# Reordering the setup of a four-layer cross-attention kernel on one core

## What is computed

```python
x = L0(x, ctx)        # layernorm of x and ctx, 8 heads, residual
x = L1(x, ctx, mask)  # 16 heads, causal and key padding mask, residual
x = L2(x, ctx)        # 16 heads, output projection, MLP with tanh gelu
x = L3(x, ctx, pad)   # masked self attention, cross attention, MLP, layernorms
```

## Time and profile before

| | us |
|---|---|
| median of 3 runs | 562.75 |
| lowest and highest | 554.84, 569.61 |
| the profiled execution | 558.87 |
| its span, first to last instruction | 557.1 |
| PE, DVE, ACT, POOL busy | 486.3, 407.6, 329.0, 263.4 |
| mean granted PE clock | 0.932 |

### The profile page before, as it was taken

One profiled execution on the slowest core, in us unless ns is written; L12 is line 12 of the kernel. 1 busy time (PEld: TensorE's weight loads), 2 busy tenths in 40 slices (PEclk: granted clock), 3 DMA queues, 4 the chain that ended last, 5 costly groups with the idle time before them and its releaser, 6 DMA issues.

```text
span 557.1 us, 16733 instructions
## 1 busy us (share of the span) xinstructions
PE 486.3 (87%) x6464; PEld 299.2 (54%) x6464; DVE 407.6 (73%) x1093; ACT 329.0 (59%) x662; POOL 263.4 (47%) x334
## 2 busy tenths in 40 slices
PE   1548876799999878899999999999999999999973
PEld 1436554455555544455666666565555556666652
DVE  6267876645688886687888877778878897788452
ACT  1424655433556554467777766656666767888851
POOL 3585776824666774524344433334333533422243
PEclk9977889965799996799999999999999999999998
DMA  4593323332233332232223322232333332220000
GB/s 112 99 274 100 103 60 96 81 72 62 64 68 86 76 78 54 59 77 69 69 67 69 69 62 60 54 70 63 77 69 85 80 79 60 69 62 14 13 20 19
DMA packets 72021, 40.68 MB, mean 73 GB/s; under 512 B 7016, under 2 KB 71560, under 8 KB 71816
## 3 DMA queue, kind: packets, MB, share of 16 engines
q1 hardware_dynamic: 71944, 39.61, 30.1%
HBM read 5.00 MB, written 1.05 MB: 11 GB/s over the span
## 4 chain that ended last, share of the span: by engine, by line
PE 65%; POOL 9%; ACT 7%; DVE 6%; SPq 5%; issue 4%; DMA 3%; POOLq 0%; ACTq 0%; DVEq 0%
PE o_ps L963 14%; PE attn_ps L933 12%; PE misc_ps L993 5%; PE misc_ps L984 5%; PE misc_ps L895 5%; PE misc_ps L970 4%; PE misc_ps L901 4%; PE misc_ps L896 3%; PE score_ps L816 3%; PE misc_ps L980 2%; POOL probs L533 2%; PE misc_ps L976 2%; POOL rest L521 2%; PE misc_ps L912 2%; POOL terms L523 2%
## 5 line engine op out<-in xcount | busy, mean ns | idle before, releaser
L745 DVE TENSOR_REDUCE max_words<-score_ps 128x4 f32<-128x512 f32 x288 | 195.8, 685 | 67.7 <-PE score_ps L849 66.1
L645 ACT ACTIVATE probs<-attn_ps 128x512 f32<-128x512 f32 x288 | 169.8, 596 | 110.5 <-PE attn_ps L933 107.2
L963 PE MATMUL o_ps<-probs,v 128*32 128x128 f32 x2304 | 127.0, 294 | 12.6 <-POOL probs L533 8.0
L849 PE MATMUL score_ps<-pairs 52*128 52x128 bf16 (+1 forms) x1152 | 118.7, 226 | 9.1 <-DMA pairs<-terms 9.1
L521 POOL TENSOR_TENSOR rest<-qk_f,terms 128x512 f32<-128x512 f32 x40 | 46.2, 1155 | 162.3 <-ACT terms L596 162.3
L933 PE MATMUL attn_ps<-pairs 55*128 55x128 bf16 (+1 forms) x1152 | 117.8, 225 | 1.9 <-issue 1.0
L933 PEld LDWEIGHTS attn_ps<-pairs 55*128 55x128 bf16 (+1 forms) x1152 | 66.7, 97 | 49.9 <-issue 34.1
L963 PEld LDWEIGHTS o_ps<-probs,v 128*32 128x32 f32 x2304 | 46.3, 110 | 60.0 <-issue 16.9
L849 PEld LDWEIGHTS score_ps<-pairs 52*128 52x128 bf16 (+1 forms) x1152 | 69.8, 98 | 11.0 <-DMA pairs<-terms 9.5
L533 POOL TENSOR_SCALAR_AFFINE_SELECT probs<-probs 128x512 f32<-128x512 f32 x64 | 39.9, 635 | 22.4 <-ACT probs L645 22.4
L527 POOL TENSOR_TENSOR terms<-rest,terms 128x512 bf16<-128x512 f32 x40 | 46.8, 1170 | 1.9
(11 more groups left out here) (104 smaller groups left out, 766.8 us busy)
## 6 DMA issues: line engine op xcount, KB each, us to landing
pairs<-terms SPq DMA_DIRECT2D x240, 128.0 KB
w<-in_weights_dram SPq DMA_DIRECT2D x1, 1984.0 KB, 8.8
x_tok<-in_x_dram SPq DMA_DIRECT2D x8, 128.0 KB, 3.2
c_tok<-in_ctx_dram SPq DMA_DIRECT2D x8, 128.0 KB, 3.3
pairs<-max_rows SPq DMA_DIRECT2D x64, 12.0 KB
out_dram<-x_tok SPq DMA_DIRECT2D x8, 128.0 KB, 1.8
pairs<-constant_rows SPq DMA_DIRECT2D x4, 112.0 KB
row<-in_rows_dram SPq DMA_DIRECT2D x1, 320.0 KB, 4.4
```

The source lines that it names most:

```text
L645: act.activation(probs[n % PROBS_RING][:, :, :].rearrange("p h q -> p (h q)"), attn_ps[n % 2][:, :], ACT.Exp, scale=float(D // HEADS[part] ...
L745: dve.tensor_reduce(max_words[ub(step) % 2][:, QUAD * g:QUAD * (g + 1)], score_ps[n % 2][:, :].rearrange("p (h k) -> p h k", h=QUAD), AX_X ...
L849: return pe.matmul(score_ps[NUM[step] % 2][:, j * S:(j + 1) * S], tile[score_rows(u), QUAD * g + j, 0, b * S:(b + 1) * S], tile[score_rows ...
L963: last = pe.matmul(o_ps[32 * j:32 * j + 32, region * P:(region + 1) * P], values, probs[n % PROBS_RING][:, j, :], start=part == L0 or g % ...
```

## The change

Setup steps are put in another order, in three places. No computation is added or taken away.

- DVE: the value memsets move from behind `ln_in` of unit 0 to behind `ln_norm` of unit 0.
- SP: with load 2 only the four fills of `pairs8` remain. The mask inputs come with load 4, the large weights with load 5 instead of load 4, and each of the fills of `pairs16` behind one of loads 4, 5, 6 and 7.
- POOL: the mask step of set s moves from position 8s - 13 to 8s + 20. In POOL's own order, masks 0, 1 and 2 then stand between `rest` and `term1` of units 5, 6 and 7; masks 3, 4 and 5 behind `term2` of units 8, 9 and 10; mask 6 between the fourth and the fifth `causal` of unit 8, and mask 7, with the masks of L3, between the fourth and the fifth `causal` of unit 9. Before, mask s stood ahead of `rest` of unit s + 1 (s up to 6), and mask 7 ahead of `rest` of unit 9.

```diff
 PREPARE = {
     L0: (("load", -43), ("ln_in", -32), ("raw_tr", -30), ("ln_norm", -31), ("ln_tr", -26), ("qk", -23),
-         ("split", -23), ("rest", -21), ("term1", -19), ("term2", -19), ("v", -16), ("mask", -13)),
+         ("split", -23), ("rest", -21), ("term1", -19), ("term2", -19), ("v", -16), ("mask", 20)),
...
-                    for r in range(RING):
-                        tile, base = pairs16[r // 2], HALF * (r % 2) + product_rows(SETS)
-                        sp.dma_start(tile[base:base + MASK_ROWS + TERMS, :, :, :].rearrange("p h a n -> p h (a n)"),
-                                     constant_rows[:, :, :, :].rearrange("p a b n -> p (a b n)").unsqueeze(1)
-                                     .to_broadcast([MASK_ROWS + TERMS, 16, 2 * TOK])).then_inc(fill16_landed, 16)
+                if step.kind == "load" and u == 4:
                     sp.dma_start(validt_raw[:, :], valid_t).then_inc(masks_landed, 16)
                     sp.dma_start(valid_raw[:, :, :], valid.partition_broadcast(P)).then_inc(masks_landed, 16)
                     sp.dma_start(padt_raw[:, :], pad_t).then_inc(masks_landed, 16)
                     sp.dma_start(pad_raw[:, :], pad.partition_broadcast(P)).then_inc(masks_landed, 16)
-                if step.kind == "load" and u == 4:
+                if step.kind == "load" and u == 5:
 
                     sp.dma_start(w[:, W_FIRST:, :], weights[:, W_FIRST:, :]).then_inc(weights_landed, 16)
+                if step.kind == "load" and u >= SETS - RING:
+
+                    r = u % RING
+                    tile, base = pairs16[r // 2], HALF * (r % 2) + product_rows(SETS)
+                    sp.dma_start(tile[base:base + MASK_ROWS + TERMS, :, :, :].rearrange("p h a n -> p h (a n)"),
+                                 constant_rows[:, :, :, :].rearrange("p a b n -> p (a b n)").unsqueeze(1)
+                                 .to_broadcast([MASK_ROWS + TERMS, 16, 2 * TOK])).then_inc(fill16_landed, 16)
...
-                if kind == "ln_in" and u == 0:
-
-                    for ring in range(RING):
-                        dve.memset(v8[ring][:, :], 1.0)
-                        dve.memset(v16[ring][:, :, :], 0.0).then_inc(v_zeroed, 1)
-                    dve.wait_ge(v_zeroed, RING)
-                    for ring in range(RING):
-                        dve.memset(v16[ring][:, 0:PAIR * 16, 24:25], 1.0)
...
+                if kind == "ln_norm" and u == 0:
+
+                    for ring in range(RING):
+                        dve.memset(v8[ring][:, :], 1.0)
+                        dve.memset(v16[ring][:, :, :], 0.0).then_inc(v_zeroed, 1)
+                    dve.wait_ge(v_zeroed, RING)
+                    for ring in range(RING):
+                        dve.memset(v16[ring][:, 0:PAIR * 16, 24:25], 1.0)
```

## The result

The changed kernel takes 576.23 us (median of 4 runs, 574.60 to 578.13) against 564.10 for the kernel before (median of 4 runs, 554.84 to 569.61). The ratio is 1.0313, with an interval from 1.0175 to 1.0452: slower, though whether by more than 2% is not certain, where no change was forecast; the time is above the range of 551 to 573. Its profiled execution took 574.60 us (span 572.9) against 558.87 (span 557.1), so 15.7 us are to be found.

What follows compares the result with a forecast made beforehand. Transfers bound the start, later PE at its granted clock. Start -3.0, L0 -3.4, clock -1.0, mask 6 0, mask 7 +5.2 and low clock +1.6 gave -0.6: 562 us from the median of 562.75, range 551 to 573.

Steps and rivals of the forecast that it cites:

- L0 without masks on POOL: In L0, masks no longer delay `rest`: 3.4 us gained, made of 4.2 at L755 less 0.2 lost each time at L705.
- A: Theory of the experiments, not sized in the forecast: in L0 POOL's `rest` and DVE's normalisation meet.
- C: Theory of the experiments: mask 7 stands between unit 9's causals; forecast at 5.2 us of wait plus 1.6 of low clock.
- Memsets: At the start, the first normalisation begins at 6.84, 4.36 us earlier, but `rest` of unit 0 only 1.46 us earlier.
- First and second scores: At the start, SP's new order brings PE's first scores at 25.3 (5.2 us gained), second at 33.8 (7.1 gained).
- The weights hold the maximum: At stack 2, the large weights delay unit 0's second maximum; PE waits 3.8 us, leaving the start a gain of 3.0.
- Rival 1: At the start, the weights don't hold the small DMA, so 7.1 us stay gained: 558.1 us, chance 0.2.
- Mask 7: In unit 9 of L1, mask 7 between causals makes PE wait: +5.2 us, from +3 to +6.7.
- Low clock: PE falls to the low clock for 7 us behind mask 7, +1.6 us; less low clock in L0 gains 1.
- Rival 4: In L0, `rest` and L705 shut each other out in four units, +2.6 us: 564.8 us, chance 0.13.
- Rival 3: Behind mask 7 in unit 9, PE has the low clock for 27 us, costing 6.2: 576.3 us, chance 0.1.
- B: Theory of the experiments: the large weights stand ahead of the maximum's DMA; forecast as a 3.8 us wait of PE.

Runs made afterwards that it cites:

- e4: The changed kernel with `rest` in L0 waiting for the next unit's normalisation: 564.97 us, ratio 1.0135 to the kernel before.
- e7: The kernel before with only the memsets moved behind the first normalisation: 555.26 us, ratio 0.9992 to the kernel before.
- e5: e4 with the mask steps at 8s + 8 instead of 8s + 20: 556.63 us, ratio 0.9991 to the kernel before.
- e2: The changed kernel with the large weights behind load 7 instead of load 5: 574.41 us, ratio 1.0324 to the kernel before.
- e1: The changed kernel with the mask steps at 8s + 8 instead of 8s + 20: 572.68 us, no ratio given.
- e6: e5 with the large weights behind load 3 instead of load 5: 552.85 us, ratio 0.9868 to the kernel before.
- e3: The kernel before with only the mask steps moved to 8s + 20: 572.14 us, ratio 1.0259 to the kernel before.
- e8: The kernel before with only SP's DMA order changed (fills, mask inputs, weights): 567.71 us, ratio 1.0167 to the kernel before.
- e9: e6 with its `v16` memsets spread behind the normalisations of units 4 to 7: 555.55 us, ratio 0.9893 to the kernel before.
- e10: e6 unchanged, measured again in more runs: 552.04 us, ratio 0.9845 to the kernel before.

## Why the prediction was wrong

It failed mainly at one step, **"L0 without masks on POOL"**, and there at the sentence that prices `rest` beside L705 at "0.2 us lost each time by that row". The row, 0.78 us, was of L705 beside a mask instruction. Beside `rest` and the terms the normalisations of a unit take up to 3.9 us instead of 1.1 (32.12 to 36.04 in after), and they stand on PE's path, ahead of the transposes. e4, which removes only that, gives back 9.5 us by unit 8. By unit 8 the forecast had -7.4 and the measurement +4.7, 12.1 us apart: A is 9.5 of them. The other 2.6 are sizes of the start: e4 is 4.8 us ahead of before, not 7.4, and its third scores are 0.6 early, not 3.3. Behind unit 8 the forecast had +6.8, which C met, against 10.4: it put a longer low clock at the turn to L1 at nothing.

By its steps:

- **Memsets**: the first normalisation came at 6.40 (6.84 forecast). That `rest` of unit 0 would come 1.5 us earlier was near (2.2: 18.31 to 16.10). Not seen was that it then starts together with the normalisation of unit 1: the clash is in e7 too, and alone costs nothing.
- **First and second scores**: 27.34 and 36.79, against 25.3 and 33.8. With the clash gone they are at 25.56 and 36.01. So the SP step was right for stack 0, and stack 1 landed 2.2 us later than worked out: its last DMA was issued by 32.4 in e4, where the forecast had an issue end near 30.
- **The weights hold the maximum**: right in mechanism, and near in size once the normalisations are short (3.32 to 3.43 us in e4 and e5, 3.8 forecast); in after it was 6.10, and the large DMA took 11.9 us to land instead of the 8.8 of the earlier trace rows. Rival 1, that they wouldn't hold it, fell; e2 shows the same hold at another place. The third scores were 4.2 us late (50.28 to 54.52) instead of 3.3 early, and 0.6 early in e4.
- **L755**: right. From 42 to 86 us it had 6.6 us in 8 instructions; in after 8 of them from 46 to 96 us have 2.3. The gain of 4.2 came and was spent several times over by L700: in the window from 14 to 96 us the normalisations rose from 9.3 to 19.6 us while L755 fell from 9.9 to 2.8 (12 and 11 instructions).
- **Masks 3 to 6**: right at 0. **Mask 7**: right, 5.29 us where 5.2 were forecast, and 7.0 (e1) or 6.8 (e4 to e5) with the low clock behind it against 6.8.
- **Low clock**: units 8 to 13 took 10.4 us more, of which C explains 7.0. The other 3.4 are in e1, e5 and e6 as well (63.7 us against 60.3 in before). There the clock is low for 41.0 us in one piece between units 8 and 13; in before it is low for 30.7, in pieces of 3.4 (from 112.1) and 27.3. The 10.3 us more, at a loss of 1 - 11.48/14.92 = 0.23, are 2.4 us. e7, with no low clock there, takes 51.6 us for the same units, which makes the loss 0.28 ((60.3 - 51.6) / 30.7), and 2.9 us. So 0.5 to 1.0 of the 3.4 us stays unexplained. For L0 the forecast had 1 us gained by less of it; up to unit 8 the clock was low for 23.9 us in before and 27.3 in after, 0.8 us lost at 0.23.
- **Rival 4** named the mechanism, from the Trainium skill (SBUF — State Buffer, Who interferes with whom), and was given 0.13 and 2.6 us, against a row of another operation. Its bound, one `rest` of 1.15 us to wait for, was too low: three instructions of POOL follow each other, 16.10 to 19.59, and DVE's four took until 19.92; and it met in six units, not four. The trace agrees with the rule in that what meets is held: 1.12 us of DVE work took 3.76 beside 3.49 of POOL, and `rest`, where it came second at 26.02, took 1.30 instead of 1.15. That a shared port is the reason is what the Trainium skill says; e4 shows only that the cost goes when the two no longer meet.
- **Rival 3** gave 576.3, almost the time measured, by another way: it wanted the low clock for 27 us behind mask 7. After PE's wait the clock was low for 6.8 us, to 173.1 (0.74 from 160 to 173 us, 1.00 from 173 to 187), close to the 7 us of the forecast itself. A rival that meets the number for a wrong reason proves nothing.

Put together on the spans: A 9.5, C 7.0 and the 3.4 that go with the longer low clock make 19.9; the rest of the change gives back 4.8 by unit 8 (e4, with B's wait of 3.3 us still in it) and there is 0.6 of difference behind unit 13: 19.9 - 4.8 + 0.6 = 15.7. This sum closes because of how it is made: 4.8 and 3.4 are what A and C leave of their stretches. A and C were removed by experiments; that the 3.4 belong to the change, and not to which execution was profiled, is not shown.

Left open: what decides whether the low clock comes at the turn to L1, and for how long. Its longest piece was 27.3 us in before, 41.0 in e1, e3 to e6, e8 and e9, 51.2 in e10; in after it came in several, the longest 23.9; and e7's profiled execution had none, as its window shows:

```profile
119.00:146.00 27.00, 23.31 (x390) 13.51 (x391) 21.93 (x52) 14.08 (x28) 15.76 (x22) 1.00 0.33 74
```

The kernel before alone differs as much among its runs of one chip: 553.53 us at a mean clock of 0.954 and 552.43 at 0.950, 561.19 and 560.30 at 0.926. No experiment was aimed at it.

## What to carry to other kernels

Before moving work off an in-order engine, ask what it kept apart there: look at which instructions of the other engines begin once the moved one no longer stands between them, and price that meeting by a row of the same two operations, or take the whole length of what runs beside it as the bound. Where a rule names the very pair of instructions that the edit brings together and the only row against it is of another pair, the rule's case should hold the greater chance. And a DMA that is large against its neighbours belongs where its queue has a hole, not merely later: with load 5 PE waited 3.4 us for the small DMA behind it (e5), with load 7 5.8 (e2), with load 3 not at all at that place (e6), and unit 8 came 5.1 us earlier.

## What was not expected of the hardware

- A pair of f32 tensor_scalar instructions of 128x128 on DVE took 0.60 us alone, 0.78 beside POOL's small mask instructions, and up to 2.43 beside POOL's tensor_tensor instructions of 128x512 (`rest` and the terms). POOL's own stayed at 1.15 where they began first or together, and took up to 1.30 where DVE was under way.
- A DMA of 12 KB that follows one of 1984 KB on the same queue, with a fill of 112 KB and two stacks of 128 KB between them, kept PE waiting for 3.3 to 6.1 us (e4, e5, e2, after); with the large one issued at 10.65, 22 us ahead of the first small one, and fill and stacks where they were, the longest such wait was 0.66 us (e6).
- The low clock at the turn to L1 had a piece of 27.3 us in before, with PE busy for 26.4 of 27 us in it, of 41.0 or 51.2 in most of the others, and none in e7 (1.00 from 119 to 146 us, PE busy for 23.3 of 27), whose edit concerns the first 14 us alone.
